# The last residual of a routed decoder layer, added in the expert stage by VectorE instead of being stored and read back

## The chip, the cores and the metric

The kernel runs on one core of a Trainium2 chip, as one launch. A core has five engines with queues of their own: TensorE (PE in the profile, with PEld for its weight loads), VectorE (DVE), ScalarE (ACT), GpSimd (POOL) and SyncE (SP, which here only issues transfers). They share the on-chip memory SBUF, TensorE writes its results into PSUM, and 16 DMA engines move data between SBUF and HBM. Engines wait for each other by semaphores. The metric is the device time of one execution in microseconds; lower is better.

## The reference

Input `x` is 32 sequences of 256 tokens of 256 numbers. Three parts follow one another, each with a residual and a layer norm behind it: a Mamba-like mixer, a cross attention on 77 context rows, and a layer of 8 experts of which every token takes 2. The change touches the last part and the norm behind it:

```python
def _L0_ffn_ref(x, gate_w, w1, b1, w2, b2, ln_g, ln_b):
    ...
    scores = xt @ gate_w
    ew, ei = jax.lax.top_k(scores, K)                 # K = 2
    ew = jax.nn.softmax(ew, axis=-1)                  # the two shares of a token add up to 1
    wE = jnp.sum(ew[None, :, :] * mask, axis=-1)
    h = jax.nn.gelu(jnp.einsum('td,edf->etf', xt, w1) + b1[:, None, :], approximate=False)
    o = jnp.einsum('etf,efd->etd', h, w2) + b2[:, None, :]
    y = _layernorm(xt[None, :, :] + o, ln_g[:, None, :], ln_b[:, None, :])     # eps 1e-6
    out = jnp.einsum('et,etd->td', wE, y)
    ...
x = _layernorm(x + _L0_ffn_ref(x, ...), axis=-1)      # eps 1e-5; this x is x2 in the kernel
```

## The kernel before

The program is five stages, each a block of its own with a queue written out per engine: the mixer, keys and values of the context, the attention (`attention_phase`), the experts (`experts_phase`) and the last norm (`finish_phase`). A stage starts when every engine has left the one before.

**Attention.** It goes over the 32 sequences. At its end `normalise` writes the normed rows x2 into `x2_t`, together with four numbers per row: the token's number, its first expert, and the two shares in the form "more" and "less". SyncE's `store` writes the 256 columns of x2 to a scratch tensor in HBM, and GpSimd scatters the whole row of 260 numbers (`sent_scratch`) twice, to the place of each of its two experts.

**Experts.** The scattered rows are worked off in 71 tiles of 256 rows, each for one expert. `run_steps` gives every engine a list of (function, lag): in step s the function works on tile s minus lag, in the order of the list. A loop of X tiles stands between eight steps in front and some steps behind that are written out. Per tile:
- SyncE loads the rows into `xa`, which has X = 4 slots (`load_rows`, three tiles ahead), and the first weight of the expert into `w1`, which has 2 slots (`load_w1`, two tiles ahead; 1,024 KB a tile). `load_rows` for tile t+3 waits until tile t-1 has given its slot back (L1946 to L1949), and `load_w1` stands behind it in the same queue.
- TensorE turns the rows (`turn_x`), multiplies by w1 (`up`) and by w2 (`down`, one tile behind). Each product is made of three matmuls of rounded high and low halves (`split3`, L112 to L114).
- ScalarE writes the high halves (`x_high`, `h_high`), does the gelu, and scales the finished rows by the share over the deviation (`scale_out`, L2060, three tiles behind).
- VectorE writes the low halves (`h_low` L2087, `x_low` L2075), and two tiles behind adds residual and down product, takes mean and variance, and multiplies by the gain (`centre`, L2116 to L2131). `shares` (L2096 to L2106) works out each row's share and its place in `made_scratch`.
- GpSimd adds b2 to the rows (`add_b2`, L2148), scatters the scaled rows (`send_back`, L2171) and raises the variance to the power -1/2 (`scale`, L2156, L2161).

**Last norm.** It goes over the 32 sequences with four slots. SyncE loads the two scaled rows of every token (`d_got`) and x2 (`d_xr`); GpSimd adds the two (`join`, L2335); TensorE makes the shares times the experts' ln_b (`shifts`, L2262); VectorE adds that to x2 (L2302), adds the joined rows (L2309) and takes mean and variance; GpSimd makes the deviation (L2342, L2346) and ScalarE writes the result, which SyncE stores.

Of the kernel before, what the change touches and what calls it, by code (L numbers as in the profile page):

```python
# [1202 lines left out]
def attention_phase(nc, n_seq, signals, x1, keys, values, x2, weights, head, proj, w2, rows_in, routing):  # L1203
# [15 lines left out]
    with ExitStack() as ctx:  # L1219
# [79 lines left out]
        s_vv_in, s_x2_out = ([sem(f"{n}{i}") for i in range(2)] for n in ("vv_in", "x2_out"))  # L1299
# [570 lines left out]
def experts_phase(nc, signals, done_with, routing, b1, weights, w2):  # L1870
# [5 lines left out]
    X = 4  # L1876

    with ExitStack() as ctx:
# [187 lines left out]

        @block.vector
        def _(dve):
# [40 lines left out]
            def centre(t):  # L2109
# [16 lines left out]
                dve.tensor_scalar(ve[:, t.par, :], mv[:, t.par, :, 1], LN_E, None, ALU.add).then_inc(s_ve, 1)  # L2126
# [300 lines left out]
```

## Time and profile before

| what | value |
|---|---|
| median of three runs | 2399.41 us (2393.7 to 2405.24) |
| the profiled execution's own time | 2397.11 us |
| its span, first to last instruction | 2395.3 us |
| granted TensorE clock, mean | 0.941 |
| busy over the span: PE, DVE, ACT, POOL | 90%, 71%, 63%, 48% |
| attention, stretch 830 to 1700 us | PE busy 844.12 of 870 us |
| expert stage, first to last `h_low` | 1788.6 to 2260.9 us |
| last norm, first adding to the end | 2286.8 to 2395.3 us |

The profile is one execution. A row of a timeline gives start, duration, engine, source line, operation, the tile it writes, the tiles it reads and how many were merged; in brackets stands how long the engine was idle before it and what ended that. SPq is SyncE's queue, where an issued transfer shows, not its landing. A row of one tile gives the minimum, median and maximum duration in ns and the first and last start.

### The profile page before, as it was taken

The page shows a single profiled execution, that of the slowest core. Times are in us where ns is not written, and L with a number is a line of the kernel's source. Part 1 is how long each engine was busy: PE and PEld are TensorE (multiplying, and loading weights), DVE is VectorE, ACT ScalarE, POOL GpSimd, SP SyncE. Part 2 cuts the span into 40 slices and gives each one's busy share as a digit, 9 for nine tenths or more (in the row PEclk, how much of TensorE's full clock was granted, in tenths as well). Part 3 has the DMA queues.
Part 4 walks back from the last instruction along what each step waited for, and adds up shares of the span by engine and source line. Part 5 has one row for each costly group of instructions (what it writes and reads, how often), then busy time and mean ns, then how long its engine had stood idle before and what let it go on. Part 6 is the DMA issues. An engine that isn't in the chain of part 4 may idle for free. (4 is left out here: it accounts for less than half of the span.)

```text
span 2395.3 us, 53622 instructions
## 1 busy us (share of the span) xinstructions
PE 2148.7 (90%) x15740; PEld 1907.7 (80%) x15741; DVE 1698.7 (71%) x4406; ACT 1505.1 (63%) x3174; POOL 1158.1 (48%) x1379
## 2 busy tenths in 40 slices
PE   6998998998986989999999999999949999999776
PEld 5777887887876878888888888888848998889733
DVE  6877777877875325677767777776747777777678
ACT  6777777777774326666666666666626655556533
POOL 2655655555554002334334434343336767766655
PEclk8999999999997999999999999999979999999955
DMA  4111111111110551332232223222157777777588
GB/s 141 53 35 35 35 33 37 35 31 35 35 31 32 187 203 62 96 101 80 83 92 79 83 79 97 78 81 82 64 190 230 232 229 230 236 228 236 163 300 267
DMA packets 185344, 278.70 MB, mean 116 GB/s; under 512 B 26092, under 2 KB 107508, under 8 KB 185268
## 3 DMA queue, kind: packets, MB, share of 16 engines
q1 hardware_dynamic: 171220, 241.04, 32.2%
q0 software_dynamic: 12960, 35.67, 4.0%
q10 hardware_dynamic: 1088, 1.07, 0.1%
q8 instruction: 37, 0.61, 0.1%
q14 instruction: 39, 0.32, 0.0%
HBM read 184.33 MB, written 93.38 MB: 116 GB/s over the span
## 5 line engine op out<-in xcount | busy, mean ns | idle before, releaser
L1556 ACT ACTIVATE b_wk_f<-b_ps_s,b_nmx 128x77 f32<-128x77 f32 x1024 | 234.7, 349 | 16.2 <-DVE b_nmx L1604 16.2
L604 DVE SCALAR_TENSOR_TENSOR a_conv<-a_xc_pad,a_cw,a_conv 128x256 f32<-128x256 f32 x384 | 221.0, 636 | 1.7 <-ACT a_conv L478 1.7
L1564 ACT ACTIVATE b_pT<-b_ps_pT 77x1024 f32<-77x1024 f32 x128 | 130.8, 1022 | 142.1 <-PE b_ps_pT L1462 142.1
L2043 ACT ACTIVATE c_hid<-c_ps_h,c_b_c 128x256 f32<-128x256 f32 x284 | 111.5, 476 | 144.8 <-issue 85.4
L112 PE MATMUL c_ps_h<-c_xT_hi,c_w 128*128 128x256 f32 x568 | 166.6, 293 | 37.6 <-DMA c_b_c<-in_c_b 32.6
L2171 POOL DMA_INDIRECT made_scratch<-c_o_s,c_to x142 | 146.0, 1028 | 96.8 <-ACT c_o_s L2060 42.0
L1620 DVE TENSOR_TENSOR k_wk_lo<-b_ps_oT,k_wk_lo 128x512 fp32r<-128x512 f32 x128 | 88.0, 687 | 128.9 <-ACT k_wk_lo L1570 128.9
L1547 ACT ACTIVATE b_qT<-b_ps_q,b_bq_s 128x256 f32<-128x256 f32 x256 | 107.7, 472 | 106.7 <-PE b_ps_q L114 105.1
L2087 DVE TENSOR_TENSOR c_h_lo<-c_hid,c_h_hi 128x1024 fp32r<-128x1024 f32 x71 | 100.3, 1412 | 99.1 <-ACT c_h_hi L2052 67.7
L1849 POOL CAST w<-k_c_f 128x256 f32 (+1 forms) x32 | 13.3, 416 | 315.9 <-DMA k_c_f<-in_c_w 315.9
L112 PE MATMUL c_ps_o<-w,c_h_hi 128*128 x568 | 159.0, 280 | 3.5 <-DVE c_h_lo L2087 3.5
L1450 PE MATMUL b_ps_s<-b_kz,b_qT 128*128 128x154 f32 x1024 | 156.2, 294 | 5.3 <-ACT b_wk_f L1556 5.2
L113 PE MATMUL c_ps_h<-c_xT_lo,c_w 128*128 128x256 f32 x568 | 160.8, 283 | 0.0
L114 PE MATMUL c_ps_h<-c_xT_hi,c_w 128*128 128x256 f32 x568 | 160.6, 283 | 0.0
L114 PE MATMUL c_ps_o<-w,c_h_lo 128*128 x568 | 158.7, 279 | 0.0
L113 PE MATMUL c_ps_o<-w,c_h_hi 128*128 x568 | 158.7, 279 | 0.0
L112 PE MATMUL b_ps_q<-k_wk_hi,b_wq_hi 128*128 128x256 f32 x512 | 155.0, 303 | 2.4 <-DVE k_wk_hi L1596 1.5
L112 PE MATMUL b_ps_out<-b_wo_hi,k_wk_lo 128*128 128x256 f32 x512 | 156.1, 305 | 0.0
L1841 POOL DMA_INDIRECT sent_scratch<-b_x_t,b_pos x128 | 127.6, 997 | 47.1 <-issue 47.1
L1450 PEld LDWEIGHTS b_ps_s<-b_kz,b_qT 128*128 128x128 f32 x1024 | 140.4, 189 | 6.1 <-issue 6.0
L112 PEld LDWEIGHTS c_ps_h<-c_xT_hi,c_w 128*128 128x128 f32 x568 | 108.3, 191 | 45.9 <-issue 24.4
L113 PE MATMUL b_ps_q<-k_wk_hi,b_wq_hi 128*128 128x256 f32 x512 | 144.2, 282 | 0.0
(286 smaller groups left out, 7788.8 us busy)
## 6 DMA issues: line engine op xcount, KB each, us to landing
c_w<-parts_scratch SPq DMA_DIRECT2D x71, 1024.0 KB
c_xa<-sent_scratch SPq DMA_DIRECT2D x71, 260.0 KB, 3.1
d_got<-made_scratch SPq DMA_DIRECT2D x32, 512.0 KB, 5.0
keys_scratch<-k_k_s SPq DMA_DIRECT2D x8, 1232.0 KB, 4.7
b_kz<-keys_scratch SPq DMA_DIRECT2D x64, 154.0 KB, 2.8
b_vv<-values_scratch SPq DMA_DIRECT2D x32, 308.0 KB
a_xT_f<-in_xT SPq DMA_DIRECT2D x32, 256.0 KB, 3.1
a_x_f<-in_x SPq DMA_DIRECT2D x32, 256.0 KB, 2.7
```

The costliest lines, as they stand in the source:

```text
L112: eng.matmul(out, lh, rh, start=start, stop=False)
L113: eng.matmul(out, lh, rl, start=False, stop=False)
L114: return eng.matmul(out, ll, rh, start=False, stop=stop)
L604: dve.scalar_tensor_tensor(out=conv[:, m, :], in0=xc_pad[:, m, k:k + L], scalar=cw[:, m, k:k + 1], in1=conv[:, m, :], op0=ALU.mult, op1=AL ...
L1450: last = pe.matmul(s_scores[:, i, 2 * j:2 * j + 2, :], qT[:, u.par, i, P * j:P * j + P], kz[:, b.par, :, GM * g + i, :], start=True, stop= ...
L1547: last = act.activation(qT[:, u.par, i, :], ps_q[:, L * i:L * i + L], ACT.Identity, bias=bq_s[:, m:m + 1], scale=HD ** -0.5)
L1556: last = act.activation(pe_[:, u.par, c, :], s_scores[:, c // (C // GM), c % (C // GM), :], ACT.Exp, bias=nmx[:, u.par, c:c + 1])
L1564: act.activation(pT[:, u.par, :, :], ps_pT[0:LK, :, :], ACT.Copy).then_inc(s_pTc, 1)
L1841: pool.indirect_dma_start(routing.sent, bass.IndirectOffsetOnAxis(pos[:, b.par, 2 * c + n:2 * c + n + 1], 0), x2_t[:, b.par, c, :], None). ...
L2043: last = act.activation(hid[:, T * m:T * m + T], ps_h[t.par][:, m // 2, T * (m % 2):T * (m % 2) + T], ACT.Gelu, bias=b1_c[:, t.par, m:m + 1])
L2087: dve.tensor_tensor(h_lo[:, t.par, :], hid[:, :], h_hi[:, t.par, :].bitcast(F32), ALU.subtract).then_inc(s_hlo, 1)
L2171: pool.indirect_dma_start(routing.made, bass.IndirectOffsetOnAxis(to[:, t.slot, c:c + 1], 0), o_s[:, t.par, c, :], None).then_inc(s_sent[t ...
```

## The change

- The expert stage's rows come back with the residual in them. Since each token comes back twice, and the two are added, the sum would hold x2 twice; so everything else is doubled too and the last norm's epsilon is multiplied by four, which leaves the norm's result as it was. The doubling of the shares is a factor 0.25 on the variance before the power -1/2; the doubling of the ln_b part is `scale=2.0` in `take_w`.
- ScalarE's `scale_out` is gone. VectorE's `add_x` does the same multiplication and adds the rows of `xa` in one instruction for each 128 rows, three tiles behind, between `x_low` and `centre`.
- `xa` is thus read two tiles longer. It gets 8 slots in place of 4, and the loop of the stage holds 8 tiles.
- x2 is neither stored in the attention nor loaded in the last norm, and the last norm's VectorE has one instruction over both halves in place of four.

```diff
@@ attention_phase @@
-            def store(b):
-                sp.wait_ge(s_x2, b.count(NT, NT))
-                sp.dma_start(rows(x2, b), x2_t[:, b.par, :, 0:D]).then_inc(s_x2_out[b.par], 16)
...
-            run_steps(sp, n_seq, [(load_keys, 0), (load_xa_ahead, 0), (load_values_next, 0), (load_later, 0), (load_part, 0), (store, 3),
+            run_steps(sp, n_seq, [(load_keys, 0), (load_xa_ahead, 0), (load_values_next, 0), (load_later, 0), (load_part, 0),
                                   (store_part, 1)],
...
             def normalise(b):
                 dve.wait_ge(s_rs, b.count(1, 1))
                 if not b.before(2):
-                    dve.wait_ge(s_x2_out[b.par], b.half * 16)
                     dve.wait_ge(s_scat[b.par], b.half * (16 * 2 * NT))
@@ experts_phase @@
-    X = 4
+    X = 8
...
                     sp.wait_ge(s_x, t.ago(X).count(1, 1))
+                    sp.wait_ge(s_os, t.ago(X).count(1, 1))
                 sp.dma_start(xa[:, t.slot, :, :], tile_rows(routing.sent, r)).then_inc(s_xa_in[t.slot], 16)
...
-            def scale_out(t):
-                act.wait_ge(s_rw, t.count(1, 1))
-                act.wait_ge(s_t, t.count(NT, NT))
-                if not t.before(2):
-                    act.wait_ge(s_sent[t.par], t.half * (16 * NT))
-                for c in range(NT):
-                    last = act.activation(o_s[:, t.par, c, :], tt[:, t.par, c, :], ACT.Copy,
-                                          scale=rw[:, t.par, c:c + 1])
-                last.then_inc(s_os, 1)
-
             x_high(Item(0, 0, X))
-            run_steps(act, n_tiles, [(x_high_next, 0), (scale_out, 3), (gelu, 0), (h_high, 0)], spare=3, per=X, peel=8)
+            run_steps(act, n_tiles, [(x_high_next, 0), (gelu, 0), (h_high, 0)], spare=3, per=X, peel=8)
...
-                dve.tensor_scalar(ve[:, t.par, :], mv[:, t.par, :, 1], LN_E, None, ALU.add).then_inc(s_ve, 1)
+                dve.tensor_scalar(ve[:, t.par, :], mv[:, t.par, :, 1], LN_E, 0.25, ALU.add, ALU.mult).then_inc(s_ve, 1)
...
+            def add_x(t):
+                dve.wait_ge(s_rw, t.count(1, 1))
+                dve.wait_ge(s_t, t.count(NT, NT))
+                if not t.before(2):
+                    dve.wait_ge(s_sent[t.par], t.half * (16 * NT))
+                for c in range(NT):
+                    last = dve.scalar_tensor_tensor(out=o_s[:, t.par, c, :], in0=tt[:, t.par, c, :],
+                                                    scalar=rw[:, t.par, c:c + 1], in1=xa[:, t.slot, c, 0:D],
+                                                    op0=ALU.mult, op1=ALU.add)
+                last.then_inc(s_os, 1)
+
             x_low(Item(0, 0, X))
-            run_steps(dve, n_tiles, [(h_low, 1), (x_low_next, 0), (centre, 2), (shares, 1)], spare=3, per=X, peel=8)
+            run_steps(dve, n_tiles, [(h_low, 1), (x_low_next, 0), (add_x, 3), (centre, 2), (shares, 1)], spare=3, per=X, peel=8)
@@ finish_phase @@
-    LN_EPS = 1e-5
+    LN_EPS = 4 * 1e-5
...
                 if not b.before(X):
-                    sp.wait_ge(s_y, b.ago(X).count(NT, NT))
+                    sp.wait_ge(s_both, b.ago(X).count(1, 1))
                 sp.dma_start(got[:, b.slot, :, :, :].rearrange("p c n d -> p c (n d)"), of_seq(made, b)
                              ).then_inc(s_got_in[b.slot], 16)
-                sp.dma_start(xr[:, b.slot, :, :], of_seq(x2, b)).then_inc(s_xr_in[b.slot], 16)
...
-                act.activation(wT[:, b.par, :, :].rearrange("p c t -> p (c t)"), ps_w[b.par][0:E, 0:NT * P], ACT.Copy
+                act.activation(wT[:, b.par, :, :].rearrange("p c t -> p (c t)"), ps_w[b.par][0:E, 0:NT * P], ACT.Copy,
+                               scale=2.0
                                ).then_inc(s_wT, 1)
...
             def centre(b):
-                dve.wait_ge(s_xr_in[b.slot], b.turn * 16 + 16)
                 dve.wait_ge(s_b, b.count(1, 1))
-                if not b.before(1):
-                    dve.wait_ge(s_y, b.ago(1).count(NT, NT))
-                for c in range(NT):
-                    dve.tensor_tensor(y0[:, c, :], ps_b[b.par][:, D * c:D * c + D], xr[:, b.slot, c, :], ALU.add
-                                      ).then_inc(s_y0, 1)
                 dve.wait_ge(s_both, b.count(1, 1))
...
-                for c in range(NT):
-                    dve.wait_ge(s_y0, b.count(NT, c + 1))
-                    dve.tensor_tensor(yy[:, b.slot, c, :], y0[:, c, :], both[:, b.slot, c, :], ALU.add).then_inc(s_y, 1)
-                for c in range(NT):
-                    dve.wait_ge(s_y, b.count(NT, c + 1))
+                dve.tensor_tensor(yy[:, b.slot, :, :].rearrange("p c d -> p (c d)"), ps_b[b.par][:, :],
+                                  both[:, b.slot, :, :].rearrange("p c d -> p (c d)"), ALU.add).then_inc(s_y, 1)
+                dve.wait_ge(s_y, b.count(1, 1))
+                for c in range(NT):
                     dve.bn_stats(st[:, c, :], yy[:, b.slot, c, :]).then_inc(s_st, 1)
```

VectorE in the expert stage, one step of the loop before the change, from `h_low` of one tile on. The rows ISA, REGISTER_ALU and TENSOR_LOAD only wait or fetch the expert's number.

```order
L2087 TENSOR_TENSOR c_h_lo<-c_hid,c_h_hi 128x1024
L2072 REGISTER_ALU
L2075 TENSOR_TENSOR c_xT_lo<-c_ps_x,c_xT_hi 128x512
L1932 ISA
L1932 TENSOR_LOAD r_table
L1932 ISA x2
L2116 TENSOR_TENSOR c_yy<-c_ps_o,c_xb 128x256 x2
L2119 REGISTER_ALU
L2120 BN_STATS c_st<-c_yy 128x6
L2119 REGISTER_ALU
L2120 BN_STATS c_st<-c_yy 128x6
```

The same place of the changed kernel, whose lines are numbered 15 lower here:

```order
L2072 TENSOR_TENSOR c_h_lo<-c_hid,c_h_hi 128x1024
L2057 REGISTER_ALU
L2060 TENSOR_TENSOR c_xT_lo<-c_ps_x,c_xT_hi 128x512
L2124 ISA
L2126 SCALAR_TENSOR_TENSOR c_o_s<-c_tt,c_rw,c_xa 128x256 x2
L1926 ISA
L1926 TENSOR_LOAD r_table
L1926 ISA x2
L2101 TENSOR_TENSOR c_yy<-c_ps_o,c_xb 128x256 x2
L2104 REGISTER_ALU
L2105 BN_STATS c_st<-c_yy 128x6 x2
```

Two instructions on two halves stand new between `x_low` and `centre`, and read `c_tt`, `c_rw` and `c_xa`; nothing else moves. On ScalarE the two instructions of L2060 are gone and the rest closes up.

VectorE in the last norm, one sequence in the loop before the change:

```order
L2322 SCALAR_TENSOR_TENSOR d_nm<-d_mv,d_rs 128x2
L2298 REGISTER_ALU
L2302 TENSOR_TENSOR d_y<-d_ps_b,d_xr 128x256 x2
L2308 REGISTER_ALU
L2309 TENSOR_TENSOR d_yy<-d_y,d_both 128x256
L2308 REGISTER_ALU
L2309 TENSOR_TENSOR d_yy<-d_y,d_both 128x256
L2312 BN_STATS d_st<-d_yy 128x6 x2
L105 MEMSET d_spare 1x1
L2316 BN_AGGR d_mv<-d_st 128x2 x2
```

The same place now:

```order
L2309 SCALAR_TENSOR_TENSOR d_nm<-d_mv,d_rs 128x2
L2291 REGISTER_ALU
L2295 TENSOR_TENSOR d_yy<-d_ps_b,d_both 128x512
L2299 BN_STATS d_st<-d_yy 128x6 x2
L104 REGISTER_ALU
L105 MEMSET d_spare 1x1
L2303 BN_AGGR d_mv<-d_st 128x2 x2
```

Four additions of 256 columns, two from PSUM and two from SBUF alone, became one of 512 columns that reads PSUM and `d_both`.

## Rows read from the trace of the kernel before

**Rows 1.** Windows: stretch, length, busy us by engine (instructions), granted clock, DMA share, GB/s.
```profile
830.00:1700.00 870.00, 844.12 (x6743) 746.80 (x6741) 580.15 (x1603) 563.12 (x1558) 303.16 (x492) 0.99 0.29 93
1970.00:2030.00 60.00, 55.26 (x469) 54.64 (x468) 46.53 (x143) 36.46 (x73) 40.71 (x43) 1.00 0.71 225
2300.00:2350.00 50.00, 39.02 (x93) 19.36 (x93) 47.18 (x151) 20.62 (x46) 34.20 (x46) 0.50 0.97 320
```

**Rows 2.** Waits of PE, expert stage (1800 to 2266): total us, times, longest.
```profile
PE c_ps_h L112 <- DMA c_b_c<-in_c_b: 32.6, 27, 2.6
```

**Rows 3.** Waits of SyncE's queue, same stretch.
```profile
SPq L1948 <- DVE c_share L2106: 222.7, 65, 5.3
```

**Rows 4.** Timeline 2000 to 2013: a gelu, the loads behind it, and a late `up`.
```profile
2000.73 1.57 ACT L2043 ACTIVATE c_hid<-c_ps_h,c_b_c 128x256 f32<-128x256 f32 x4 [1.36 <-PE c_ps_h L114]
...
2003.79 0.38 SPq L1950 DMA_DIRECT2D c_xa<-sent_scratch  x1
2005.14 0.37 SPq L1957 DMA_DIRECT2D c_w<-parts_scratch  x1
2005.70 0.36 SPq L1960 DMA_DIRECT2D c_b_c<-in_c_b  x1
...
2012.58 0.36 PE L112 MATMUL c_ps_h<-c_xT_hi,c_w 128*128 128x256 f32 x1 [2.55 <-DMA c_b_c<-in_c_b]
```

**Rows 5.** Timeline of one step, 2003.5 to 2009.3: VectorE, GpSimd, ScalarE.
```profile
2003.51 1.23 DVE L2087 TENSOR_TENSOR c_h_lo<-c_hid,c_h_hi 128x1024 fp32r<-128x1024 f32 x1
2004.65 0.68 DVE L2075 TENSOR_TENSOR c_xT_lo<-c_ps_x,c_xT_hi 128x512 fp32r<-128x512 f32 x1
2005.45 0.76 DVE L2116 TENSOR_TENSOR c_yy<-c_ps_o,c_xb 128x256 f32<-128x256 f32 x2
...
2007.40 0.88 DVE L2131 SCALAR_TENSOR_TENSOR c_tt<-c_yy,c_mv,b_w_stage 128x256 f32<-128x256 f32 x2
2008.20 0.22 DVE L2096 TENSOR_SCALAR c_move<-c_xa,r_own 128x2 f32<-128x2 f32 x1
...
2008.65 0.15 DVE L2106 TENSOR_TENSOR c_share<-c_part,c_xa 128x2 f32<-128x2 f32 x1
...
2003.73 1.06 POOL L2161 TENSOR_TENSOR c_rw<-c_rs,c_share 128x2 f32<-128x2 f32 x1 [0.16 <-POOL c_rs L2156]
2004.75 1.29 POOL L2148 TENSOR_TENSOR c_xb<-c_xa,b_w_stage 128x512 f32<-128x512 f32 x1
2006.74 1.04 POOL L2171 DMA_INDIRECT made_scratch<-c_o_s,c_to  x1 [0.70 <-issue]
...
2009.14 0.73 POOL L2156 TENSOR_TENSOR c_rs<-c_ve,c_pow_half 128x2 f32<-128x2 f32 x1
...
2004.98 0.91 ACT L2060 ACTIVATE c_o_s<-c_tt,c_rw 128x256 f32<-128x256 f32 x2 [0.41 <-POOL c_rw L2161]
```

**Rows 6.** One tile's rows: `h_low` here, and the mixer's scalar_tensor_tensor.
```profile
L2087 DVE TENSOR_TENSOR c_h_lo<-c_hid,c_h_hi x71: 1224/1226/2322, 1788.6 to 2260.9; 128x1024 fp32r<-128x1024 f32 x71
...
L604 DVE SCALAR_TENSOR_TENSOR a_conv<-a_xc_pad,a_cw,a_conv x384: 470/479/1268, 18.0 to 723.1; 128x256 f32<-128x256 f32 x192
```

**Rows 7.** Last norm: L2309's row, then the timeline near 2331 and TensorE's near 2298.
```profile
L2309 DVE TENSOR_TENSOR d_yy<-d_y,d_both x64: 407/417/1548, 2287.4 to 2389.0; 128x256 f32<-128x256 f32 x64
...
2331.09 1.84 DVE L2309 TENSOR_TENSOR d_yy<-d_y,d_both 128x256 f32<-128x256 f32 x2
...
2331.38 1.27 POOL L2335 TENSOR_TENSOR d_both<-d_got 128x512 f32<-128x512 f32 x1
...
2297.19 2.07 PE L2262 MATMUL d_ps_b<-d_shift,d_wT 8*128 8x256 f32 x4
...
2299.71 2.07 PE L2262 MATMUL d_ps_b<-d_shift,d_wT 8*128 8x256 f32 x4
```

**Rows 8.** DMA issues: tile, queue, count, KB each, median us to landing.
```profile
d_got<-made_scratch SPq DMA_DIRECT2D x32, 512.0 KB, 5.0
...
d_xr<-x_scratch SPq DMA_DIRECT2D x32, 256.0 KB, 5.1
```

More of the change, by code:

```diff
@@ L1200, in _, with attention_phase @@
             done_with.clear(pool)
-def attention_phase(nc, n_seq, signals, x1, keys, values, x2, weights, head, proj, w2, rows_in, routing):
+def attention_phase(nc, n_seq, signals, x1, keys, values, weights, head, proj, w2, rows_in, routing):
     LK, HD, DH, MH = proj.LK, proj.HD, proj.DH, proj.MH
@@ L1298, in attention_phase @@
         s_xa_in, s_kz_in = proj.s_xa_in, proj.s_kz_in
-        s_vv_in, s_x2_out = ([sem(f"{n}{i}") for i in range(2)] for n in ("vv_in", "x2_out"))
+        s_vv_in = [sem(f"vv_in{i}") for i in range(2)]
         s_ahead, s_cut_hi, s_cut_lo = sem("ahead"), sem("cut_hi"), sem("cut_lo")
@@ L1402, in _ @@
             for par in (0, 1):
-                sp.wait_ge(s_x2_out[par], 16 * (n_seq // 2))
                 sp.wait_ge(s_cut_out[par], 16 * (n_seq // 2))
@@ L2176, in _, with finish_phase @@
                 pool.wait_ge(s_sent[par], 16 * NT * ((n_tiles + 1 - par) // 2))
-def finish_phase(nc, n_seq, signals, routing, x2, rows, masks, out):
-    LN_EPS = 1e-5
+def finish_phase(nc, n_seq, signals, routing, rows, masks, out):
+    LN_EPS = 4 * 1e-5
     with ExitStack() as ctx:
@@ L2193, in finish_phase @@
         shift = sb("shift", [E, D])
-        xr = sb("xr", [P, X, NT, D])
         got = sb("got", [P, X, NT, 2, D])
         both = sb("both", [P, X, NT, D])
-        y0 = sb("y0", [P, NT, D])
         wT = sb("wT", [E, 2, NT, P])
@@ L2213, in finish_phase @@
         s_c, s_one, s_ve = sem("const"), sem("one"), sem("ve")
-        s_xr_in, s_got_in, s_o_out = ([sem(f"{n}{i}") for i in range(X)] for n in ("xr_in", "got_in", "o_out"))
-        s_both, s_y0 = sem("both"), sem("y0")
+        s_got_in, s_o_out = ([sem(f"{n}{i}") for i in range(X)] for n in ("got_in", "o_out"))
+        s_both = sem("both")
         s_w, s_wT, s_b, s_y, s_st, s_mv, s_rs, s_nm, s_ot = (
@@ L2259, in shifts @@
                 if not b.before(2):
-                    pe.wait_ge(s_y0, b.ago(2).count(NT, NT))
+                    pe.wait_ge(s_y, b.ago(2).count(1, 1))
                 for c in range(NT):
@@ L2333, in join @@
                 if not b.before(X):
-                    pool.wait_ge(s_y, b.ago(X).count(NT, NT))
+                    pool.wait_ge(s_y, b.ago(X).count(1, 1))
                 pool.tensor_tensor(both[:, b.slot, :, :], got[:, b.slot, :, 0, :], got[:, b.slot, :, 1, :], ALU.add
@@ L2353, in program @@
     x1 = nc.dram_tensor("x1_scratch", [n_seq * L, D], F32).ap()
-    x2 = nc.dram_tensor("x2_scratch", [n_seq * L, D], F32).ap()
     keys = nc.dram_tensor("keys_scratch", [n_seq, P, Projections.MH * Projections.LK], F32).ap()
@@ L2371, in program @@
                     keys_values_phase(nc, n_seq, in_b, in_a, head, weights, proj, w2, routing, keys, values, x1)
-                attention_phase(nc, n_seq, in_b, x1, keys, values, x2, weights, head, proj, w2, c_rows, routing)
+                attention_phase(nc, n_seq, in_b, x1, keys, values, weights, head, proj, w2, c_rows, routing)
             experts_phase(nc, in_c, in_b, routing, c_b1, weights, w2)
-        finish_phase(nc, n_seq, in_d, routing, x2, c_rows, masks, out)
+        finish_phase(nc, n_seq, in_d, routing, c_rows, masks, out)
 def layouts(inputs):
```

## The prediction

> **What bounds the kernel now.** I read the windows first, one per stage, because the change touches three stages with different limits [rows 1]. In the attention TensorE is busy 844.12 of 870 us: nothing but TensorE sets the pace there. In the expert stage it is busy 55.26 of 60 us at full clock, VectorE 46.53, the DMA engines 0.71. In the last norm VectorE is busy 47.18 of 50 us and the DMA engines 0.97 at 320 GB/s, while TensorE stands at half clock (0.50, the 1.2 GHz level).
>
> The spacing of the tiles in the expert stage comes from `h_low`, which runs once per tile: (2260.9 - 1788.6) / 70 = 6.75 us [rows 6]. Per tile TensorE is busy 6.75 x 55.26 / 60 = 6.2 us, VectorE 6.75 x 46.53 / 60 = 5.2 us. So TensorE leads, with about half a microsecond of waiting per tile. The waits say for what: 32.6 us in 27 pieces for `c_b_c`, the transfer behind the first weight [rows 2]. Why that one is late stands in SyncE's queue: it waits 222.7 us for `c_share` of VectorE, 65 times [rows 3]. The timeline shows one case [rows 4]: the gelu ends at 2002.30 and frees the weight's slot, but the queue still holds `load_rows`, which waits for the share of an earlier tile (written at 2008.65 in the next step, so once a step, at its end) [rows 5]; the rows are issued at 2003.79, the weight at 2005.14, and a later `up` begins 2.55 us late at 2012.58.
>
> The spacing in the last norm: L2309 starts first at 2287.4 and last at 2389.0; the last is a second half, some 0.3 us behind its first, so (101.6 - 0.3) / 31 = 3.27 us per sequence [rows 7].
>
> **Part 1, x2 is no longer stored in the attention.** 32 issues and 32 x 256 KB of writing go, with DMA share 0.29 and TensorE 97% busy [rows 1]. The two ends are 0 and the whole 26 us in which TensorE was not busy; I take 0, since a TensorE that is held by its own matmuls in 97% of the time has nothing to gain from a store. The buffer of x2 is still held by the scatter.
>
> **Part 2, eight slots for the rows.** `load_rows` for tile t+3 now waits for tile t-5, which is long done. The weight behind it is issued when the gelu ends, up to 2.8 us sooner [rows 4]. If nothing else changed, TensorE's waits for weights would go and the spacing would fall to TensorE's busy time, 6.2 us: 70 x (6.75 - 6.2) = -38 us. That is the offer; part 3 decides how much of it is taken.
>
> **Part 3, the scaling moves from ScalarE to VectorE.** ScalarE loses 0.91 us per tile, which frees nobody: it isn't late. VectorE gets two scalar_tensor_tensor on 256 columns with both tensors in SBUF. The same kind, `c_tt`, takes from its start to the next instruction 2008.20 - 2007.40 = 0.80 us for two [rows 5]. VectorE's step without a wait goes from 2003.51 to the end of the share at 2008.80, 5.29 us. With add_x it is 6.09 us, about TensorE's 6.2. So the slack that VectorE had is spent, and any hold on VectorE now counts.
>
> There is such a hold. `h_low` takes 1,224 ns in most cases and up to 2,322, and the mixer's scalar_tensor_tensor takes 470 to 1,268 ns [rows 6]; in the last norm two additions of SBUF tensors take 1.84 us instead of about 0.8 while GpSimd's `join` runs (2331.38 for 1.27 us), and the second ends just behind it [rows 7]. In the other direction `c_rw`, a 128x2 operation, takes 1.06 us since it lies beside `h_low` [rows 5]. The two engines take turns when both read from SBUF with two tensors, for a whole instruction. The Trainium skill says the same (SBUF — State Buffer, "Who interferes with whom"): a VectorE instruction with two SBUF inputs and a GpSimd instruction that reads SBUF exclude each other, and whoever issued first runs to its end. The trace agrees, and by that rule add_x is among those held.
>
> Where does `add_x` fall? I place it by the step in [rows 5], counting from `h_low`'s start. `add_x` wants to begin where `c_yy` begins now, at 1.94, or up to 0.2 sooner. GpSimd's `c_rw` is let in when `h_low` ends, and `add_b2` follows at 1.24 and runs to 2.53. So `add_x` waits from 1.94 (or 1.75) to 2.53, 0.6 to 0.8 us; I take 0.65. Is that a passing accident or does it come back? ScalarE's scaling ends at 2005.89 and the power behind the scatters at 2009.87, so GpSimd reaches `c_rw` 3.98 us after the scaled rows are ready. With the wait, add_x ends at about 3.4, `c_rw` is ready at 7.4, and the next `h_low` starts at 6.09 + 0.65 = 6.74: again `c_rw` comes while `h_low` runs, and `add_b2` right behind it. Without the wait it would be 2.8 + 3.98 = 6.8 against 6.09, and it would also come beside `h_low`. The collision repeats. Spacing then is 6.74 us, VectorE is the bound, and the offer of part 2 is used up by it. The two ends for the wait are 0 (spacing 6.2, TensorE's) and the whole 1.29 us of `add_b2` (7.38). I take 6.70, a little under 6.74 because now and then GpSimd is held up by its own scatters: 70 x (6.70 - 6.75) = -3.5 us. In this the older holds on `h_low` are not counted twice: with VectorE bound, `add_b2` always comes after it.
>
> **Part 4, the last norm.** Per sequence VectorE loses two additions from PSUM (as `c_yy`, 0.76 us the pair [rows 5]) and two from SBUF (0.83 to 1.84 us the pair [rows 7]), and gets one of 512 columns from PSUM and SBUF, as `x_low`, 0.68 us [rows 5]. Its 47.18 / 50 x 3.27 = 3.08 us fall to 1.2 to 2.2 us. The new addition has one SBUF input, and `c_yy` and `x_low`, of that kind, show no such hold in rows 5. The transfers fall from 512 + 256 + 256 KB to 512 + 256 KB (the result is as large as x2) [rows 8]: 786,000 bytes at the 320 GB/s of rows 1 are 2.46 us. What is late next is TensorE: undisturbed it gives a new `d_ps_b` every 2299.71 - 2297.19 = 2.52 us [rows 7], at the low clock. GpSimd needs 34.20 / 50 x 3.27 = 2.24 us. Three needs within 0.3 us of each other do not interlock without loss, and the small instruction that makes the negated mean still has two SBUF inputs beside `join`; I take 2.65 us. 31 x (3.27 - 2.65) = -19 us, with the ends -23 (2.52) and -7 (3.05, where VectorE and `join` still hold each other for a large part).
>
> The stage's start and end, the eight written-out steps and the barrier are as before; the longer loop body costs nothing that a row shows, and I take 0.
>
> **Sum.** -3.5 - 19 = -23 against the profiled execution's 2397.1 us gives 2374; its span is 2395.3, so 1.8 us lie outside and stay. The median of the runs is 2.3 us above that execution, which would give 2377. I write 2375.
>
> **The rivals.**
> - *VectorE and GpSimd do not collide in the long run.* For it: GpSimd's place in the step moves with each scatter, and the 6.09 us of VectorE fit under TensorE's 6.2. Against it: the arithmetic above, by which it falls back beside `h_low`. Spacing 6.2 to 6.3: 70 x 0.5 = -35, with the last norm -54: about 2343.
> - *The expert stage becomes slower (the other sign).* Place: GpSimd between `c_rw` and `add_b2`. If GpSimd is some 0.6 us later than computed, because scatters wait for earlier ones to land, `add_b2` begins just before `add_x` and holds it for all of its 1.29 us; spacing 6.09 + 1.29 = 7.38, +44 us, with the last norm +25: 2422. It decides against the kernel from a spacing of 6.75 + 19 / 70 = 7.02. Against it: a later VectorE gives GpSimd time to catch up.
> - *The last norm does not get shorter by much.* For it: the DMA engines are at 0.97 and could be held by packets rather than bytes. Spacing 3.05, -7 us, expert stage 0: 2390. Against it: VectorE's rows of 1.84 us and the removed bytes both point to less.
>
> **How the numbers follow.** The forecast 0.57, no collision 0.17, slower expert stage 0.10, little gain in the last norm 0.16. About 0.5% (12 us) is what a measurement can tell from no change, so faster means under 2387.4 against the median of 2399.4. The forecast's own range is 2362 to 2388 and lies almost wholly in it. Faster: nearly all of 0.57, 0.17, and 0.03 of the last rival, 0.76. Same: 0.16, most of the last rival and the edges of its neighbours. Slower: 0.08. The range of 8 in 10 is 2342 to 2399.
>
> **What would show it.** The waits of SyncE's queue for `c_share` gone. The weight issued within 0.3 us of the gelu's end. TensorE waiting for `c_h_lo` instead of for `c_b_c`. `c_o_s` rows on VectorE of 1.1 us and more beside `c_xb`, and `h_low` starts 6.7 us apart with VectorE's idle gaps nearly gone. In the last norm, yy of about 0.68 us without long ones, and 2.65 us per sequence with TensorE hardly waiting. If the expert stage is at 6.2 us or `c_o_s` never takes longer than 0.5 us, part 3's collision is wrong; if the last norm stays above 3 us, part 4 is.

## The result, and the profile after

The changed kernel takes 2366.74 us (median of 4 runs, 2364.66 to 2369.48), the kernel before 2400.43 us beside it: ratio 0.9862, 95% interval 0.9836 to 0.9889. That is 33.7 us less; 2375 us was forecast, in a range of 2342 to 2399. The profiled execution is the longest of its four, 2369.48 us with a span of 2367.7, which is 27.6 us less than the profiled one of before.

The windows of the changed kernel, in the columns of [rows 1]:

```profile
830.00:1700.00 870.00, 843.75 (x6733) 746.68 (x6734) 581.41 (x1605) 560.95 (x1557) 306.44 (x492) 0.99 0.26 84
1970.00:2030.00 60.00, 56.51 (x464) 55.20 (x463) 51.91 (x162) 28.75 (x54) 45.69 (x45) 1.00 0.74 237
2290.00:2340.00 50.00, 50.00 (x121) 24.75 (x120) 35.32 (x140) 26.64 (x60) 42.17 (x61) 0.50 0.94 296
```

The attention is as it was, only its DMA share is 0.26 instead of 0.29. In the expert stage VectorE went from 46.53 to 51.91 of 60 us, and TensorE is still not full. In the last norm TensorE now fills the window, at half clock, and VectorE fell from 47.18 to 35.32.

The rows by tile name that carry the spacings (duration min/median/max in ns, first and last start in us), which answer to [rows 6] and [rows 7]:

```profile
L2072 DVE TENSOR_TENSOR c_h_lo<-c_hid,c_h_hi x71: 1210/1224/2151, 1793.0 to 2255.7; 128x1024 fp32r<-128x1024 f32 x71
L2126 DVE SCALAR_TENSOR_TENSOR c_o_s<-c_tt,c_rw,c_xa x142: 470/482/1510, 1807.8 to 2269.1; 128x256 f32<-128x256 f32 x142
L2295 DVE TENSOR_TENSOR d_yy<-d_ps_b,d_both x32: 690/692/693, 2283.5 to 2361.0; 128x512 f32<-128x512 f32 x32
```

Expert stage: (2255.7 - 1793.0) / 70 = 6.61 us per tile instead of 6.75, which is -9.6 us over the stage. Last norm: (2361.0 - 2283.5) / 31 = 2.50 us per sequence instead of 3.27, which is -24 us. The first `h_low` begins 4.4 us later than before, 1793.0 against 1788.6, with the same work ahead of it but for the store; in six other kernels with just that work (e4, e5, e8 and e10 to e12 below) it began between 1782.6 and 1796.0, so this is scatter between executions. -9.6 - 24 + 4.4 = -29, against -27.6 measured.

The waits of the changed kernel in the expert stage (stretch 1800 to 2262 of its profile; total us, times, longest), which answer to [rows 2] and [rows 3]:

```profile
DVE c_o_s L2126 <- POOL c_rw L2157: 42.1, 67, 2.6
...
PE c_ps_o L112 <- DVE c_h_lo L2072: 20.9, 25, 3.0
...
POOL made_scratch L2167 <- DMA made_scratch<-c_o_s,c_to: 16.8, 15, 1.7
```

```profile
SPq L1951 <- ACT c_hid L2038: 223.1, 67, 5.2
```

The wait for `c_b_c` is gone and so is the one of SyncE's queue for the share: its only wait is now for the gelu, as it should be. In their place VectorE waits for `c_rw` of GpSimd in nearly every tile. The timeline of the changed kernel shows first a step with a long wait and then the next one, with a short wait (start, duration, engine, line, operation; in brackets the idle time before and what ended it):

```profile
2043.80 1.04 POOL L2167 DMA_INDIRECT made_scratch<-c_o_s,c_to  x1 [0.83 <-DMA made_scratch<-c_o_s,c_to]
...
2045.03 1.22 DVE L2072 TENSOR_TENSOR c_h_lo<-c_hid,c_h_hi 128x1024 fp32r<-128x1024 f32 x1
2045.14 1.95 POOL L2167 DMA_INDIRECT made_scratch<-c_o_s,c_to  x1 [0.30 <-DVE c_share L2091]
2046.17 0.68 DVE L2060 TENSOR_TENSOR c_xT_lo<-c_ps_x,c_xT_hi 128x512 fp32r<-128x512 f32 x1
2047.11 0.74 POOL L2152 TENSOR_TENSOR c_rs<-c_ve,c_pow_half 128x2 f32<-128x2 f32 x1
2047.92 0.20 POOL L2157 TENSOR_TENSOR c_rw<-c_rs,c_share 128x2 f32<-128x2 f32 x1
2048.25 0.88 DVE L2126 SCALAR_TENSOR_TENSOR c_o_s<-c_tt,c_rw,c_xa 128x256 f32<-128x256 f32 x2 [1.40 <-POOL c_rw L2157]
...
2048.86 1.42 POOL L2144 TENSOR_TENSOR c_xb<-c_xa,b_w_stage 128x512 f32<-128x512 f32 x1 [0.74 <-issue]
...
2052.82 1.23 DVE L2072 TENSOR_TENSOR c_h_lo<-c_hid,c_h_hi 128x1024 fp32r<-128x1024 f32 x1 [0.35 <-issue]
2052.83 1.81 POOL L2152 TENSOR_TENSOR c_rs<-c_ve,c_pow_half 128x2 f32<-128x2 f32 x1
2054.71 0.19 POOL L2157 TENSOR_TENSOR c_rw<-c_rs,c_share 128x2 f32<-128x2 f32 x1
2055.15 0.88 DVE L2126 SCALAR_TENSOR_TENSOR c_o_s<-c_tt,c_rw,c_xa 128x256 f32<-128x256 f32 x2 [0.50 <-POOL c_rw L2157]
```

In the first of the two steps there are three things to see. The first scatter of this tile starts only when the scatters of the tile before have landed. The second is held by `h_low` (1.95 us instead of 1.04). And the power and `c_rw`, for which `add_x` waits, stand behind both in GpSimd's order (`add_b2`, `send_back`, `scale`). `add_x` itself is not held: `add_b2` begins 0.61 us behind its start (and takes 1.42 us where [rows 5] had 1.29).

The second step is the more frequent kind. Its scatters are out before `h_low` begins, but the power starts while `h_low` runs and is held by it (1.81 us instead of 0.73), so `c_rw` is again too late, by less. Counted over the steps of tiles 8 to 61: in 42 of 54 the power starts inside `h_low` and `add_x` waits 0.3 to 0.5 us, 15.7 us together; in 11 it starts behind `h_low` and `add_x` waits 1.3 to 2.6 us, 16.7 us together.

### The profile page after: what moved, and what is told of

Read it like the earlier page. It is cut to its first block and busy times, and to the rows that moved or that the text cites. A ratio compares the mean times of both kernels' runs of the same rounds, so it can differ in the third digit from the quotient of the medians.

```text
span 2367.7 us, 52943 instructions
## 1 busy us (share of the span) xinstructions
PE 2160.6 (91%) x15740; PEld 1921.0 (81%) x15741; DVE 1704.4 (72%) x4452; ACT 1444.5 (61%) x3032; POOL 1178.9 (50%) x1379
## 5 line engine op out<-in xcount | busy, mean ns | idle before, releaser
L112 PE MATMUL c_ps_o<-w,c_h_hi 128*128 x568 | 165.7, 292 | 23.4 <-DVE c_h_lo L2072 23.0
L2167 POOL DMA_INDIRECT made_scratch<-c_o_s,c_to x142 | 153.7, 1082 | 62.6 <-issue 32.5
L113 PE MATMUL c_ps_o<-w,c_h_hi 128*128 x568 | 160.9, 283 | 0.0
L112 PE MATMUL b_ps_out<-b_wo_hi,k_wk_lo 128*128 128x256 f32 x512 | 156.3, 305 | 0.0
L114 PE MATMUL b_ps_q<-k_wk_hi,b_wq_lo 128*128 128x256 f32 x512 | 144.3, 282 | 0.0
L114 PE MATMUL b_ps_out<-b_wo_hi,k_wk_lo 128*128 128x256 f32 x512 | 142.6, 279 | 0.0
```

Source lines behind the costliest of these rows:

```text
L112: eng.matmul(out, lh, rh, start=start, stop=False)
L113: eng.matmul(out, lh, rl, start=False, stop=False)
L114: return eng.matmul(out, ll, rh, start=False, stop=stop)
L2167: pool.indirect_dma_start(routing.made, bass.IndirectOffsetOnAxis(to[:, t.slot, c:c + 1], 0), o_s[:, t.par, c, :], None).then_inc(s_sent[t ...
```

## The experiments

All times are medians, the ratio is to the kernel before beside it. "Spacing" is that of `h_low`, (last start - first start) / 70, in the one profiled execution. Three kernels with the changed expert stage as it is have 6.61, 6.57 and 6.57 (the changed one, e2, e6), two with that of before 6.75 and 6.70 (before, e3): a difference of 0.05 says nothing.

| run | ratio, 95% interval | us | spacing us |
|---|---|---|---|
| e1_slots8 | 1.0107 (1.0068 to 1.0146) | 2422.71 | 7.02 |
| e2_experts | 0.996 (0.9936 to 0.9984) | 2386.99 | 6.57 |
| e3_norm | 0.9899 (0.986 to 0.9938) | 2374.82 | 6.70 |
| e4_lag4 | 0.9808 (0.9771 to 0.9845) | 2352.04 | 6.38 |
| e5_half_b2 | 0.9847 (0.9803 to 0.9891) | 2366.05 | 6.55 |
| e6_store | 0.9845 (0.9796 to 0.9894) | 2366.93 | 6.57 |
| e7_scale_last | 1.0124 (1.007 to 1.0178) | 2431.92 | 7.13 |
| e8_lag4_free_to | 0.9783 (0.9739 to 0.9826) | 2350.15 | 6.35 |
| e9_slots8_two_made | 0.983 (0.979 to 0.987) | 2353.5 | 6.11 |
| e10_half_two_made | 0.9781 (0.9745 to 0.9817) | 2344.58 | 6.33 |
| e11_two_made | 0.9792 (0.9763 to 0.9821) | 2347.11 | 6.38 |
| e12_scale_first | 0.9749 (0.9712 to 0.9786) | 2335.31 | 6.11 |

### The parts one by one

**e1_slots8**: the kernel before, and only

```diff
-    X = 4
+    X = 8
```

> The kernel before with eight slots and a loop of eight tiles in the expert stage, nothing else. It isolates the earlier issue of the weight. If late weights were what spaced the tiles, SyncE's wait for c_share goes, the weight is issued within 0.3 us of the gelu's end, and the spacing of h_low falls from 6.75 to 6.2 us (TensorE's busy time): about 38 us less than before, some 2362 us. Rival: the weights land late anyway because the transfers themselves are slow; then the spacing stays above 6.5 us and less than 18 us is gained.

It became slower, by 23 us. The slots did what they were to do: the weight is issued 0.16 us behind the gelu (median; 1.62 us before), and TensorE's waits for `c_b_c` fell from 32.2 to 8.6 us (1800 to 2235). But the waits of e1_slots8 (1800 to 2235) show this:

```profile
ACT c_o_s L2060 <- POOL c_rw L2161: 167.0, 55, 5.4
DVE c_h_lo L2087 <- ACT c_h_hi L2052: 70.1, 60, 3.0
POOL made_scratch L2171 <- DMA made_scratch<-c_o_s,c_to: 36.1, 17, 2.5
...
POOL made_scratch L2171 <- DVE c_to L2104: 25.2, 15, 2.1
```

So eight slots alone are a loss, and something behind `c_rw` is why. Two candidates: the gelu, which stands in ScalarE's queue behind the scaling that waits for `c_rw`; or what makes `c_rw` late.

**e2_experts**: before, with the expert stage of the changed kernel (the residual is then added twice and the last norm's epsilon doesn't fit). **e3_norm**: before, with its last norm alone (the residual is left out).

> The kernel before with the changed expert stage alone: add_x on VectorE and eight slots; x2 is still stored and the last norm is the old one, so the residual enters twice and the epsilon is not scaled. The traces say 70 x (6.61 - 6.75) = -10 us, so about 2390 us. Against the run with eight slots alone, the move of the scaling to VectorE then costs about 28 us. If instead the expert stage carries most of the 34 us that the changed kernel gained, this is 2375 or less.

> The kernel before with the changed last norm alone: x2 is stored but not read, and the residual is left out. Spacing 2.52 us per sequence, TensorE's, in place of 3.27: 31 x 0.75 = 23 us less, so about 2377 us. If the sum of this and of the changed expert stage alone (-10) is less than the 34 us of the whole change, the store of x2 in the attention or the state of the stages between is worth the rest.

The parts add up: 0.996 x 0.9899 = 0.9859, the whole change 0.9862. Of e3_norm:

```profile
L2299 DVE TENSOR_TENSOR d_yy<-d_ps_b,d_both x32: 691/692/693, 2291.0 to 2368.1; 128x512 f32<-128x512 f32 x32
```

(2368.1 - 2291.0) / 31 = 2.49 us per sequence, as in the whole change, and this is -24.5 us of time.

**e6_store**: the changed kernel, with the store of x2 and its wait back in the attention.

```diff
+            def store(b):
+                sp.wait_ge(s_x2, b.count(NT, NT))
+                sp.dma_start(rows(x2, b), x2_t[:, b.par, :, 0:D]).then_inc(s_x2_out[b.par], 16)
```

> The changed kernel with the store of x2 in the attention put back (32 times 256 KB, with the wait of the normalisation for it), read by nobody. Theory 1: TensorE is held by its own matmuls there and the store costs nothing: within 3 us of the changed kernel (2364 to 2370). Theory 2: the store takes DMA time from loads that TensorE waits for: up to the 26 us in which TensorE was not busy, 2372 to 2392.

2366.93 us: no cost of the store shows. The medians differ by 0.2 us, in a ratio that is known to 0.5%; the profiles are the finer measure: TensorE is busy 843.26 of the 870 us with the store and 843.75 without, and the first `h_low` starts at 1792.0 and 1793.0.

### What holds the expert stage at 6.61 us

**e7_scale_last**: e1_slots8 with the scaling last in ScalarE's step.

```diff
-[(x_high_next, 0), (scale_out, 3), (gelu, 0), (h_high, 0)]
+[(x_high_next, 0), (gelu, 0), (h_high, 0), (scale_out, 3)]
```

> The kernel before with eight slots, as e1_slots8, and ScalarE's order turned: gelu and h_high first, the scaling of an older tile behind them. Theory 1: e1_slots8 was slower since gelu stood in ScalarE's queue behind a scaling that waited for c_rw; then the gelu no longer waits, TensorE gets its new weights in time, the spacing falls from 7.02 to 6.2-6.5 us and the time from 2423 to 2364-2386. Theory 2: e1_slots8 was slower since GpSimd's loop got longer (additions and scatters beside h_low); then the scaled rows only come later still, spacing 6.9 to 7.2 and 2415 to 2435.

7.13 us: the gelu behind the scaling is not the reason. Theory 2 has the size right, and the waits of e7_scale_last (1800 to 2235) name a third thing, the landing of scatters, 65.5 us against 36.1 in e1_slots8:

```profile
POOL made_scratch L2171 <- DMA made_scratch<-c_o_s,c_to: 65.5, 40, 3.1
```

**e4_lag4**: the changed kernel, `add_x` and `send_back` one tile later.

```diff
-(add_x, 3)  ...  (send_back, 3)
+(add_x, 4)  ...  (send_back, 4)
```

> The changed kernel with add_x and the scatter four tiles behind instead of three. Theory 1: in the changed kernel add_x waits for c_rw (42.1 us in the trace), because GpSimd makes c_rw of one tile behind the scatter of the tile before, so the two engines run in one loop of 6.6 us. With a step more in between, that wait goes; if only the loop's length was the limit, the spacing falls to TensorE's 6.2 us and the time to about 2366 - 28 = 2338 us; if GpSimd's own occupation is the limit (with its holds some 6.4 to 6.6 us), the spacing stays at 6.4 to 6.6 and the time within 10 us of the changed kernel. Theory 2, VectorE is held by GpSimd's add_b2 as the prediction had it: no change, 6.6 us, and c_o_s rows of 1 us and more.

14.7 us faster than the changed kernel, spacing 6.38; `c_o_s` waits for `c_rw` no more. Its rows:

```profile
L2126 DVE SCALAR_TENSOR_TENSOR c_o_s<-c_tt,c_rw,c_xa x142: 469/478/911, 1808.4 to 2249.4; 128x256 f32<-128x256 f32 x142
```

```profile
1970.00:2030.00 60.00, 59.73 (x496) 59.09 (x495) 58.71 (x174) 31.60 (x59) 47.16 (x49) 1.00 0.76 251
```

The wait for `c_rw` was thus a real loss and not slack. `add_x` itself is hardly ever held here either (one of its 142 rows is over 0.6 us). But VectorE is busy 58.71 of 60 us, and not all of that is work. The small instruction that hands the variance to GpSimd, 169 ns in the changed kernel (median of 71), is the one that now meets `add_b2`:

```profile
L2111 DVE TENSOR_SCALAR c_ve<-c_mv x71: 169/783/1296, 1798.3 to 2243.8; 128x2 f32<-128x2 f32 x71
```

In 59 of its 71 tiles it starts while `c_xb` runs, and each of these ends 0.02 to 0.03 us behind `c_xb`; in the changed kernel none starts there. That is 0.6 us of VectorE per tile, about the size that the prediction gave to the hold of `add_x`. By these numbers (an estimate) VectorE's step would be 6.38 x 58.71 / 60 - 0.61 = 5.6 us without it. I read it as what keeps this kernel from 6.11; no run removes it, so that is not shown.

**e8_lag4_free_to**: e4_lag4 with `(t.half - 2)` for `(t.half - 1)` in the wait of `shares` for an old scatter.

> e4_lag4 with the share's wait for an old scatter set back by two tiles more, which eight slots allow. In e4_lag4 GpSimd's scatters waited 8.7 us for c_to in 8 pieces. Theory 1: that was a wait for the landing of a scatter, and it goes: 5 to 9 us better than e4_lag4 (2343 to 2347). Theory 2: VectorE is busy 58.71 of 60 us in e4_lag4 and sets the pace, the wait was slack: 2350 to 2354, as before.

2350.15 us, spacing 6.35; the intervals of the two lie over each other. No gain that this measurement can tell.

**e5_half_b2**: a shorter loop on GpSimd. It adds b2 to the first 128 rows of a tile alone; for the others VectorE's `c_yy` reads `xa` itself, and b2 is left out of them.

```diff
-                pool.tensor_tensor(xb[:, t.par, :, :], xa[:, t.slot, :, 0:D], ...)
+                pool.tensor_tensor(xb[:, t.par, 0:1, :], xa[:, t.slot, 0:1, 0:D], ...)
```

> The changed kernel, but GpSimd adds b2 only to the first 128 rows of a tile (b2 is left out of the other 128); VectorE takes the rows themselves there. GpSimd's instruction shrinks from about 1.44 to about 0.75 us, VectorE's work is the same. Theory 1: VectorE's new step waits for c_rw because the loop on GpSimd (rw, add_b2, two scatters, rs, and back) is as long as a tile; then c_rw comes about 0.6 us sooner, the wait of c_o_s for c_rw (42.1 us) falls to under 10 us, the spacing goes from 6.61 to 6.2-6.35 us, and the kernel takes 2342 to 2352 us. Theory 2: VectorE's own work and its holds by GpSimd's additions set the pace, and the wait for c_rw is only where the slack is written down; then less than 0.1 us of spacing changes: 2358 to 2367.

Theory 1 failed as I had put it: 2366.05 us, spacing 6.55. The mean `c_xb` fell from 1440 to 891 ns and nothing was gained (the wait of `add_x` for `c_rw` fell from 39.7 to 34.2 us in this stretch); but a wait grew. The waits of e5_half_b2 (1800 to 2235):

```profile
POOL made_scratch L2168 <- DMA made_scratch<-c_o_s,c_to: 41.8, 34, 2.0
...
DVE c_o_s L2127 <- POOL c_rw L2158: 34.2, 56, 2.6
```

GpSimd is early and then waits for scatters to land: 41.8 us in place of 16.8. So a second chain of about the same length had been hidden: a scatter may start only when those of the tile before have landed. How long one scatter takes from issue to landing stands in one row; here of before, of e1_slots8 and of the changed kernel:

```profile
DMA to landing us min/median/max: 2.4/3.6/5.9
```

```profile
DMA to landing us min/median/max: 2.4/4.8/6.3
```

```profile
DMA to landing us min/median/max: 2.4/4.4/5.9
```

From a tile's first issue to the landing of its second, over tiles 8 to 61, this is on the mean 4.87, 6.25 and 5.44 us; and 8, 49 and 26 of 54 tiles (same order) start their scatters 0.8 to 0.9 us behind the landing of the tile before, which is as soon as any does. For e1_slots8: 6.25 + 0.9 = 7.15, and its spacing is 7.02.

**e9_slots8_two_made, e11_two_made, e10_half_two_made** take this wait away in the kernels e1_slots8, the changed one and e5_half_b2. The rows of odd tiles go to a second array, so that neighbours in time don't write the same one. Nobody reads that second array: the last norm of these three loads as many bytes of an earlier array instead, in two transfers, so the spacing is what to compare, and their output is not the layer's.

```diff
-                if not t.before(1):
-                    prev = t.ago(1)
+                if not t.before(2):
+                    prev = t.ago(2)
                     pool.wait_ge(s_sent[prev.par], prev.half * (16 * NT) + 16 * NT)
...
-                    pool.indirect_dma_start(routing.made, ...)
+                    pool.indirect_dma_start((routing.made, routing.made_2)[t.par], ...)
```

> e1_slots8, with the scattered rows of odd tiles written to a second memory array that nobody reads, so that a tile's scatter waits for the landing of the one two tiles back and not of the one before. The last norm reads rows of an earlier array in place of the experts' rows, same bytes. What counts is the spacing of h_low in the expert stage. In e1_slots8 29 of 54 scatters begin 0.90 us behind the landing of the one before, and first issue to landing takes 6.25 us (before: 4.87). Theory 1: that chain (landing 6.25 + 0.9 = 7.15) is what made eight slots slower than four: spacing falls from 7.02 to 6.2-6.6 us, 2365 to 2395. Theory 2: the landing is only where slack is written down and ScalarE's scaling in front of the gelu or GpSimd's holds set the pace: spacing stays at 6.9-7.1, 2412 to 2430.

> e5_half_b2 (GpSimd adds b2 to half of the rows) and the second array for odd tiles' rows together; the last norm reads other rows, same bytes. Theory 1: two loops over GpSimd are about equally long in the changed kernel, the one through its own instructions (additions, scatters, power, c_rw) and the one through the landing of scatters; e5_half_b2 shortened only the first, and waits for landings rose from 16.8 to 41.8 us. With both shortened the spacing falls from 6.61 to 6.2-6.4 us, 2345 to 2355. Theory 2: c_rw is late since h_low holds the power in front of it, whatever GpSimd has to do: the spacing stays at 6.5-6.6, 2358 to 2368.

> The changed kernel with the second array for odd tiles' rows alone (as e10_half_two_made, but GpSimd adds b2 to all rows); the last norm reads other rows, same bytes. e5_half_b2 (shorter additions alone) left the spacing at 6.60 against 6.61 us, e10_half_two_made (both) gave 6.33. Theory 1, two loops of about equal length, so that shortening one alone gives little: spacing 6.5 to 6.6, 2357 to 2367. Theory 2, the landing of scatters is the one that counts and the additions never did: 6.3 to 6.35, 2343 to 2349, as e10_half_two_made.

e9 is the clearest run of the study. The rows of e9_slots8_two_made, the tile row and the window:

```profile
L2088 DVE TENSOR_TENSOR c_h_lo<-c_hid,c_h_hi x71: 1224/1225/2147, 1785.4 to 2213.1; 128x1024 fp32r<-128x1024 f32 x71
```

```profile
1970.00:2030.00 60.00, 60.00 (x511) 60.00 (x510) 49.17 (x159) 40.45 (x79) 48.98 (x50) 1.00 0.77 254
```

From 7.02 to 6.11 us, TensorE busy for all of the 60 us, and the scaling is still on ScalarE there. It was the wait for the scatters of the tile before that made eight slots slower than four (the run takes away the wait and the shared array together), and it hid a gain of 70 x (6.75 - 6.11) = 45 us that needs nothing of part 3; a kernel whose output counts would have to read the rows back from both arrays, which was not tried.

In the changed kernel the same edit gives 6.38 (e11), and with the shorter additions 6.33 (e10). So for e11 theory 2 is the nearer: landings make 6.61 - 6.38 = 0.23 us, and the additions nothing that can be told from the scatter of spacings, with or without landings (6.38 to 6.33, 6.61 to 6.55; and the runs of the two, 2343.2 to 2348.72 and 2340.21 to 2347.09 us, overlap). But 6.38 - 6.11 = 0.27 us are left. In e11_two_made the wait for `c_rw` is smaller but in nearly every tile, and the power is long in most:

```profile
DVE c_o_s L2127 <- POOL c_rw L2158: 26.4, 67, 1.3
```

```profile
L2153 POOL TENSOR_TENSOR c_rs<-c_ve,c_pow_half x71: 731/1334/1811, 1792.8 to 2240.9; 128x2 f32<-128x2 f32 x71
```

With the landings gone, 66 of 71 powers start inside `h_low`. Each of them ends 0.58 or 0.59 us behind `h_low`'s end, however early it came, so `c_rw` is ready some 2.1 us behind `h_low`'s start in nearly every step, where VectorE is free for `add_x` at 1.8. That is why shorter additions give nothing there (in e10 the power only starts sooner inside `h_low`), and it is the mechanism of theory 2 of e10, though not with its number.

**e12_scale_first**: this rest goes with GpSimd's order, which decides what `h_low` holds. The changed kernel, with the power and `c_rw` ahead of the scatters:

```diff
-            run_steps(pool, n_tiles, [(add_b2, 1), (send_back, 3), (scale, 2)], spare=3, per=X, peel=8)
+            run_steps(pool, n_tiles, [(add_b2, 1), (scale, 2), (send_back, 3)], spare=3, per=X, peel=8)
```

> The changed kernel with GpSimd's order in a step add_b2, scale (power and c_rw), send_back instead of add_b2, send_back, scale: c_rw no longer queues behind the scatters and their waits. Theory 1 (c_rw is late because it stands behind scatters and landings): the wait of c_o_s for c_rw goes, spacing 6.2-6.45 us, 2345 to 2357, as e4_lag4. Theory 2 (GpSimd's loop is too long whatever its order, or scatters that come later in the step only move the wait): scale waits for VectorE's c_ve in the middle of a step and the scatters come later; spacing 6.6 or more, 2365 or more.

It is better than either theory said, and the fastest kernel here: 2335.31 us, 61 us below the one before beside it and 31 below the changed kernel's median (0.9749 against 0.9862; the intervals lie apart). Its tile rows, that of the power among them, its window and a piece of its timeline:

```profile
L2072 DVE TENSOR_TENSOR c_h_lo<-c_hid,c_h_hi x71: 1209/1224/2143, 1793.5 to 2221.5; 128x1024 fp32r<-128x1024 f32 x71
```

```profile
L2126 DVE SCALAR_TENSOR_TENSOR c_o_s<-c_tt,c_rw,c_xa x142: 467/475/485, 1806.7 to 2232.5; 128x256 f32<-128x256 f32 x142
L2152 POOL TENSOR_TENSOR c_rs<-c_ve,c_pow_half x71: 742/891/961, 1802.1 to 2230.6; 128x2 f32<-128x2 f32 x71
```

```profile
1970.00:2030.00 60.00, 60.00 (x510) 60.00 (x509) 58.43 (x175) 31.07 (x59) 46.60 (x48) 1.00 0.80 262
```

```profile
2028.66 1.30 POOL L2144 TENSOR_TENSOR c_xb<-c_xa,b_w_stage 128x512 f32<-128x512 f32 x1
...
2030.08 0.89 POOL L2152 TENSOR_TENSOR c_rs<-c_ve,c_pow_half 128x2 f32<-128x2 f32 x1
...
2031.05 0.20 POOL L2157 TENSOR_TENSOR c_rw<-c_rs,c_share 128x2 f32<-128x2 f32 x1
...
2031.64 1.23 DVE L2072 TENSOR_TENSOR c_h_lo<-c_hid,c_h_hi 128x1024 fp32r<-128x1024 f32 x1 [0.39 <-PE c_ps_o L114]
...
2031.92 1.85 POOL L2167 DMA_INDIRECT made_scratch<-c_o_s,c_to  x1 [0.68 <-issue]
...
2033.38 0.87 DVE L2126 SCALAR_TENSOR_TENSOR c_o_s<-c_tt,c_rw,c_xa 128x256 f32<-128x256 f32 x2
```

`c_rw` is written at 2031.25 and read at 2033.38: 2.1 us of slack where the changed kernel had none. No power starts inside `h_low` any more. `h_low` holds a scatter instead (1.85 us here), and nobody waits for that one. `c_ve` is held by `add_b2` here too (median 551 ns), but VectorE at 58.43 of 60 us has room for it. Spacing 6.11, TensorE 60.00 of 60: the stage is at TensorE's floor, though scatters still wait for landings (12.3 us, 11 times, 1800 to 2215): nobody stands behind them.

## Why the prediction was right or wrong

- **Part 1 (the store, 0)**: right, as far as e6_store can tell.
- **Part 2 (eight slots, "offer")**: its mechanism was right in each step that I named: no more waits of SyncE's queue for the share, none of TensorE for `c_b_c`, the weight 0.16 us behind the gelu. (In e1_slots8 8.6 us of waits for `c_b_c` are left.) The floor is 6.11 us, 6.2 was said. But "part 3 decides how much of it is taken" was wrong. What decides is the chain of scatters on GpSimd, which the sum did not have at all (e1 against e9: 7.02 and 6.11).
- **Part 3 (6.70, from a collision of `add_x` and `add_b2`)**: the size was near (6.61), the reason was wrong, and by my own test: `c_o_s` has a median of 482 ns, and of its 142 rows one is over 0.6 us. I placed `add_x` at 1.94 us behind `h_low` with `c_rw` taken as there, since in [rows 5] it came 1.06 us beside `h_low`. The step that failed is the 3.98 us from the scaled rows to the end of the power, taken over from a step of before with two free scatters, a free power and no wait for a landing, and `c_rw` "let in when `h_low` ends", at 1.24. In the changed kernel that stretch has a median of 5.09 us (tiles 8 to 61): the first scatter starts 1.4 us behind the scaled rows (median; 0.9 before), and mostly it is the power and not `c_rw` that lies beside `h_low`. So `c_rw` is ready at 2.1 us or later, `add_x` waits for it, and `add_b2`, which follows `c_rw` after 0.74 us of issue, can no longer be in `add_x`'s way. That the predicted wait and the real one lead to about one spacing is luck: each adds about half a microsecond to VectorE's 6 us. VectorE does get held by `add_b2` in other kernels here, but on `c_ve` (e4_lag4), an instruction that the prediction did not look at.
- **The rival "no collision"** (6.2 to 6.3, 2343) had the right half: in the changed kernel there is no collision on `add_x`, nor on `c_ve`. It had no other hold in its place, though, and so a time (2343) that the changed kernel does not reach; e10_half_two_made comes near it and e12_scale_first goes below.
- **The rival "slower"** named the wait of scatters for earlier ones to land, as what makes GpSimd late. That wait is real and is what made e1_slots8 slower; the hold of `add_x` by `add_b2` that was to follow from it did not come, and the chance of 0.10 put the wait aside where it belonged in the sum.
- **"ScalarE loses 0.91 us, which frees nobody"**: with scatters freed, true (e9 gets to 6.11 with the scaling on ScalarE). With the scatters as they are, moving it is worth (7.02 - 6.61) x 70 = 29 us. No run takes apart why; the landings of the changed kernel are shorter than those of e1_slots8, see the last section. Nor was GpSimd's new order tried in e1_slots8, so whether eight slots, that order and ScalarE's scaling would do as well is open.
- **Part 4 (2.65, -19)**: right in its mechanism, too careful by 5 us: 2.50, which is TensorE's 2.52 of [rows 7] with no loss on top. The 0.13 us that I added for three engines within 0.3 us of each other did not come. `d_yy` takes 692 ns in all 32 cases (690 to 693).
- **The sum**: -23 forecast; by spacings -9.6 - 24 = -33.6, by medians -33.7. Of the missing 11 us part 3 has 6 and part 4 has 5.

## What to carry to other kernels

A chain that runs through a DMA's landing (issue, landing, next issue) has a length of its own: write it beside each engine's busy time when you look for what is late next, and measure it again when a change moves large loads against it. When you price a hold of one engine by another, go through every instruction of both in the new phase, the smallest too: here the ones that were held were a power and a sum on 128x2 elements, and the large new one was not. Within a step of an in-order engine, put what another engine waits for ahead of what only stores: here one swapped pair gave nearly as much again as the whole change. And where an edit takes away a wait on one queue, run it alone once: eight slots were -45 or +19 us, by spacing, depending on what stood behind them.

## What the runs showed of the hardware

- **GpSimd's small instructions and its issue of a scatter are held by VectorE's `h_low`,** a tensor_tensor that reads two SBUF tensors, when they start inside it. A scatter takes 0.96 to 1.04 us to issue in most cases; the 65 of e12_scale_first that start inside `h_low` all end 0.91 to 0.95 us behind its end, and so take up to 1.95 us. One that started before `h_low` is not held (60 in e11_two_made, 0.96 to 1.21 us). The power on 128x2 elements, 0.73 us in most tiles before, ends 0.58 or 0.59 us behind `h_low`'s end in all 52 tiles of the changed kernel in which it starts inside it:

```profile
L2152 POOL TENSOR_TENSOR c_rs<-c_ve,c_pow_half x71: 724/1298/1814, 1803.1 to 2267.7; 128x2 f32<-128x2 f32 x71
```

  The Trainium skill (SBUF — State Buffer, "Who interferes with whom") says that a DMA which looks stalled by VectorE is one whose descriptors GpSimd makes, starved of the port, but also that tensor_tensor did not show this in its probe. The first the trace bears out, with about 0.9 us on a scatter that starts with `h_low`; on the second it differs, since `h_low` is a tensor_tensor.
- **The other way round, a tensor_scalar on 128x2 elements is held by GpSimd's addition.** `c_ve` takes 169 ns; where it starts while `c_xb` runs it ends 0.02 to 0.04 us behind it (59 of 71 tiles in e4_lag4, 66 of 71 in e12_scale_first).
- **A scatter's landing goes with where it lies to the 1 MB weight load.** From first issue to second landing in e1_slots8: 5.57 us (mean of 27) where it is issued 1 to 2 us behind a weight, 6.96 us (24) where 7 to 9 us behind, so that the next weight is issued while it runs. From the end of the second issue alone it is 2.62 and 4.50 us, so it is not the held issue. Before: 5.22 us (33) at 1 to 3 us behind, 4.30 us (21) at 3 to 4. In e12_scale_first: 5.24 us (34) at 1 to 2 and 4.55 us (19) at 2 to 3. This is an order in the rows and not an experiment: that the load makes the landing longer was not tested by itself.
